# Row maxima taken over every eighth query, with one store in place of a transpose and four, and an earlier load of a key difference

## The reference, cut to what matters

```
scores = einsum('bsdkg,btdk->bkgst', q, k) / sqrt(256)
w      = softmax(scores, axis=-1)
ctx    = einsum('bkgst,btdk->bkgsd', w, v)
```

## Time and profile before

| | us |
|---|---|
| median of 3 runs | 871.83 |
| the profiled execution | 866.55 |
| its span | 864.7 |
| VectorE (DVE) busy | 701.9, 81% of the span |
| TensorE matmul (PE) busy | 776.1, 90% |
| ScalarE (ACT) busy | 537.8, 62% |
| GpSimd (POOL) busy | 330.4, 38% |

### The profile page before, as it was taken

The page is one execution under the profiler, slowest core; times in us unless marked ns, Lnnn a source line. Parts: engine busy times, 40 slices in busy tenths (PEclk is TensorE's granted clock), DMA queues, the critical chain, the costliest instruction groups (busy, mean ns, idle before and its releaser), DMA issues. The chain is left out here.

```text
span 864.7 us, 18013 instructions
## 1 busy us (share of the span) xinstructions
PE 776.1 (90%) x6593; PEld 508.2 (59%) x6593; DVE 701.9 (81%) x1131; ACT 537.8 (62%) x988; POOL 330.4 (38%) x283
## 2 busy tenths in 40 slices
PE   3979999999999999999899998996668899999986
PEld 2865333333333333333388887986657587999875
DVE  4769999999999999999766676668999486666486
ACT  4527788887788888888844335445576353666442
POOL 5440444347544653021010000107787560444340
PEclk9985999999999999999999999998687699999999
DMA  6495532222222222000066000002006113444352
GB/s 240 172 217 165 191 89 52 52 52 53 51 53 52 52 52 52 16 16 17 20 202 127 2 1 13 2 1 70 5 11 270 69 63 60 123 124 134 114 161 74
DMA packets 60183, 71.16 MB, mean 82 GB/s; under 512 B 24864, under 2 KB 46496, under 8 KB 59712
## 3 DMA queue, kind: packets, MB, share of 16 engines
q1 hardware_dynamic: 56016, 59.31, 25.7%
q0 software_dynamic: 3408, 9.38, 3.1%
q10 hardware_dynamic: 672, 1.31, 0.5%
HBM read 40.47 MB, written 27.41 MB: 78 GB/s over the span
## 5 line engine op out<-in xcount | busy, mean ns | idle before, releaser
L767 ACT ACTIVATE probs_t<-psum 128x512 f32<-128x512 f32 x512 | 271.4, 601 | 65.5 <-PE psum L891 63.7
L791 DVE TENSOR_REDUCE row_max<-psum 128x1 f32<-128x1024 f32 x234 | 272.5, 1214 | 10.4 <-PE psum L879 9.9
L891 PE MATMUL psum<-QS,KS 50*128 50x512 f32 x512 | 194.5, 469 | 1.3 <-ACT probs_t L767 1.2
L879 PE MATMUL psum<-KS,QS 48*128 48x512 f32 x490 | 174.2, 457 | 13.6 <-DVE row_max L791 11.3
L701 POOL TENSOR_TENSOR lut_sum<-lut_sum,lut_tmp 128x1080 f32<-128x1080 f32 x45 | 112.3, 2496 | 131.0 <-DVE lut_tmp L822 131.0
L891 PEld LDWEIGHTS psum<-QS,KS 50*128 50x128 f32 x512 | 82.7, 188 | 135.2 <-ACT probs_t L767 127.8
L903 PE MATMUL psum<-probs_t,VS 128*32 128x512 f32 x1024 | 137.9, 611 | 1.1
L879 PEld LDWEIGHTS psum<-KS,QS 48*128 48x128 f32 x490 | 77.3, 195 | 54.0 <-DVE row_max L791 48.3
L2531 POOL DMA_INDIRECT y_rows<-y_slot,ids x39 | 37.5, 962 | 61.4 <-ACT y_slot L2594 61.1
L822 DVE TENSOR_SCALAR lut_tmp<-lut_idx,lut 128x1080 f32<-128x1080 int32 x60 | 47.5, 793 | 0.4
L1289 POOL TENSOR_TENSOR rstd<-var_eps,minus_half 128x4 f32<-128x4 f32 x8 | 8.4, 1045 | 99.9 <-DVE var_eps L1284 99.9
(11 more groups left out here) (333 smaller groups left out, 1902.1 us busy)
## 6 DMA issues: line engine op xcount, KB each, us to landing
KS<-k_rows SPq DMA_DIRECT2D x31, 192.0 KB, 4.5
QS<-q_rows SPq DMA_DIRECT2D x31, 192.0 KB, 5.0
x_rows<-zero_rows SPq DMA_DIRECT2D x1, 4992.0 KB, 17.7
x_slot<-x_rows SPq DMA_DIRECT2D x39, 128.0 KB
m_raw<-experts_w SPq DMA_DIRECT2D x2, 2432.0 KB
q_rows<-part SPq DMA_DIRECT2D x8, 512.0 KB, 5.2
y_token<-y_rows SPq DMA_DIRECT2D x8, 512.0 KB, 7.4
x_tok<-x SPq DMA_DIRECT2D x4, 512.0 KB, 8.8
```

Of the source, the lines that this page charges most:

```text
L767: nc.scalar.activation(pt[:, k % NPT, :], ring(k)[:], ACT.Exp, scale=float(E) ** -0.5).then_inc(p_ready, 1)
L791: nc.vector.tensor_reduce(out, m.psum[:, j:j + 2, :], AX_XY, ALU.max).then_inc(max_done, 1)
L879: mm = nc.tensor.matmul(bank[pair(k) + h], QS[n % NQK][rows(g, NROW), st * P:(st + 1) * P], keys, start=True, stop=True)
L891: nc.tensor.matmul(ring(k)[:], KS[n % NQK][rows(g, NAUG), t * P:(t + 1) * P], QS[n % NQK][rows(g, NAUG), half * BLK:(half + 1) * BLK], sta ...
```

## The change

The maxima of tile st are now those of queries st, st + 8, st + 16 and so on: partition p of column c holds query 8p + c. The stationary operand of a maximum therefore reads QS with a step of eight elements (32 bytes). The maxima of a partition are then 8 neighbouring queries for each head; one DMA stores the parts, and the two loads into QS take 128 pieces of 32 bytes for each row. The transpose and the clearing of `row_max` go; GpSimd works on 16 columns in place of 32. PLAIN goes from 4 to 2. KD[0] of head 0 moves from ScalarE's queue to SyncE's, ahead of `load_qk(1)`, and with it the wait for `kd_out`. `look_up(0)` takes over a wait that `turn_max(0)` had.

```diff
-        m.m_rows = nc.dram_tensor("m_rows", (B * KV, NPART, G * S), ...).ap()
+        m.m_rows = nc.dram_tensor("m_rows", (B * KV, P, NPART, G * S // P), ...).ap()
...
         act.wait_ge(kd_out, 32)
-        m.load_diff(act, 0)
+        m.load_diff(act, 0, (1,))
...
-    FIRST, PLAIN = NST + AHEAD, 4
+    FIRST, PLAIN = NST + AHEAD, 2
...
-    def load_diff(queue, n):
-        for g in range(G):
+    def load_diff(queue, n, heads=range(G)):
+        for g in heads:
...
         queue.wait_ge(mp_done, NPART * (n + 1))
-        for q in range(4):
-            queue.dma_start(m.m_rows[n].rearrange("i (c q s) -> q c i s", q=4, s=32)[q],
-                            mpt[32 * q:32 * q + NST, :, :].bitcast(F32)).then_inc(mp_out, 16)
-        queue.wait_ge(mp_out, 64 * (n + 1))
+        queue.dma_start(m.m_rows[n].rearrange("p i k -> p (i k)"), mpt[:]....bitcast(F32)).then_inc(mp_out, 16)
+        queue.wait_ge(mp_out, 16 * (n + 1))
         for g in range(G):
             queue.dma_start(QS[n % NQK][g * HEAD_ROWS + NROW:g * HEAD_ROWS + NAUG, :].bitcast(F32)
-                            m.m_rows[n, :, g * S:(g + 1) * S]).then_inc(m_in, 16)
+                            .rearrange("i (p c) -> i p c", c=NTT),
+                            m.m_rows[n].rearrange("p i k -> i p k")[:, :, g * NTT:(g + 1) * NTT]).then_inc(m_in, 16)
...
         load_qk(sp, 0, (0,))
+        sp.wait_ge(m.kd_out, 32)
+        load_diff(sp, 0, (0,))
         load_qk(sp, 1)
-        sp.wait_ge(m.kd_out, 32)
         load_diff(sp, 1)
...
-        pool.wait_ge(mt_done, n + 1)
-        nc.gpsimd.tensor_scalar(mres[:, 0, :], mT[:], -1.0, None, ALU.mult).then_inc(mres_done, 1)
+        pool.wait_ge(max_done, NST * (n + 1))
+        nc.gpsimd.tensor_scalar(mres[:], mx[:, n % 2, :], -1.0, None, ALU.mult).then_inc(mres_done, 1)
...
-        def turn_max(n):
-            ...
-            nc.vector.transpose(mT[:], mx[:, n % 2, :]).then_inc(mt_done, 1)
...
-            mm = nc.tensor.matmul(bank[pair(k) + h], QS[n % NQK][rows(g, NROW), st * P:(st + 1) * P], keys,
+            mm = nc.tensor.matmul(bank[pair(k) + h], QS[n % NQK][rows(g, NROW), :]
+                                  .rearrange("r (p c) -> r c p", c=NTT)[:, st], keys,
                                   start=True, stop=True)
```

More of the change, by code:

```diff
@@ L113, in program @@
         m.kd_rows = nc.dram_tensor("kd_rows", (KV * HD, len(K_SLOTS), BLK), F32, kind="Internal").ap()
-        m.m_rows = nc.dram_tensor("m_rows", (B * KV, NPART, G * S), F32, kind="Internal").ap()
+        m.m_rows = nc.dram_tensor("m_rows", (B * KV, P, NPART, G * S // P), F32, kind="Internal").ap()
         m.den_rows = nc.dram_tensor("den_rows", (B * KV, G * S), F32, kind="Internal").ap()
@@ L518, in attention_stage @@
     rec = at("rec_b", [P, 2, S], F32, b); b += 2 * S * 4
[L519 to L522, removed]
+    mx = at("row_max", [P, 2, NST], F32, b); b += 2 * NST * 4
+    mres = at("max_res", [P, NST], F32, b); b += NST * 4
+    mpt = at("max_parts", [P, NPART, NST], F32R, b); b += NPART * NST * 4
     den = at("den", [P, NST], F32, b); b += NST * 4
@@ L543, in attention_stage @@
         sem(n) for n in ("lut_in", "idx_in", "lut_prod", "lut_add", "f_hi", "f_lo"))
-    mx_zero = sem("mx_zero")
-    max_ps, max_done, mt_done, mp_done, mp_out, m_in = (
-        m.front_sem(n) for n in ("max_ps", "max_done", "mt_done", "mp_done", "mp_out", "m_in"))
+    max_ps, max_done, mp_done, mp_out, m_in = (
+        m.front_sem(n) for n in ("max_ps", "max_done", "mp_done", "mp_out", "m_in"))
     m.s_ps = sem("s_ps")
@@ L644, in place_max @@
         queue.wait_ge(mp_done, NPART * (n + 1))
-        for q in range(4):
-            queue.dma_start(m.m_rows[n].rearrange("i (c q s) -> q c i s", q=4, s=32)[q],
-                            mpt[32 * q:32 * q + NST, :, :].bitcast(F32)).then_inc(mp_out, 16)
-        queue.wait_ge(mp_out, 64 * (n + 1))
+        queue.dma_start(m.m_rows[n].rearrange("p i k -> p (i k)"), mpt[:].rearrange("p i k -> p (i k)").bitcast(F32)
+                        ).then_inc(mp_out, 16)
+        queue.wait_ge(mp_out, 16 * (n + 1))
         for g in range(G):
-            queue.dma_start(QS[n % NQK][g * HEAD_ROWS + NROW:g * HEAD_ROWS + NAUG, :].bitcast(F32),
-                            m.m_rows[n, :, g * S:(g + 1) * S]).then_inc(m_in, 16)
+            queue.dma_start(QS[n % NQK][g * HEAD_ROWS + NROW:g * HEAD_ROWS + NAUG, :].bitcast(F32)
+                            .rearrange("i (p c) -> i p c", c=NTT),
+                            m.m_rows[n].rearrange("p i k -> i p k")[:, :, g * NTT:(g + 1) * NTT]).then_inc(m_in, 16)
     def attend_sync(sp):
@@ L711, in max_parts @@
     def max_parts(pool, n):
-        pool.wait_ge(mt_done, n + 1)
-        nc.gpsimd.tensor_scalar(mres[:, 0, :], mT[:], -1.0, None, ALU.mult).then_inc(mres_done, 1)
+        pool.wait_ge(max_done, NST * (n + 1))
+        nc.gpsimd.tensor_scalar(mres[:], mx[:, n % 2, :], -1.0, None, ALU.mult).then_inc(mres_done, 1)
         pool.wait_ge(mres_done, n + 1)
         if n >= 1:
-            pool.wait_ge(mp_out, 64 * n)
-        nc.gpsimd.tensor_copy(mpt[:, 0, :], mres[:, 0, :]).then_inc(mp_done, 1)
+            pool.wait_ge(mp_out, 16 * n)
+        nc.gpsimd.tensor_copy(mpt[:, 0, :], mres[:]).then_inc(mp_done, 1)
         pool.wait_ge(mp_done, NPART * n + 1)
-        nc.gpsimd.tensor_tensor(mpt[:, 1, :], mres[:, 0, :], mpt[:, 0, :], ALU.subtract).then_inc(mp_done, 1)
+        nc.gpsimd.tensor_tensor(mpt[:, 1, :], mres[:], mpt[:, 0, :], ALU.subtract).then_inc(mp_done, 1)
     def attend_gpsimd(pool):
@@ L773, in attend_vector @@
         m.project_vector(dve)
-        nc.vector.memset(mx[:], 0.0).then_inc(mx_zero, 1)
-        dve.wait_ge(mx_zero, 1)
         def row_max(n, i):
@@ L780, in row_max @@
             if i == 0 and n >= 2:
-                dve.wait_ge(mt_done, n - 1)
+                dve.wait_ge(mres_done, n - 1)
             col = i % G * NTT + i // G
@@ L816, in look_up @@
                 dve.wait_ge(max_done, FIRST)
+                dve.wait_ge(m.part_lo, 3 * NB)
             if (c + 1) * PIECE > KC * GUW and v == 0:
@@ L826, in attend_vector @@
             row_max(i // NST, i % NST)
-            if i == NST - 1:
-                turn_max(0)
         for n in range(NG):
@@ L833, in attend_vector @@
                     row_max(k // NST, k % NST)
-                    if k % NST == NST - 1:
-                        turn_max(k // NST)
                 if i == 12 and n >= 1:
```

## The result

The changed kernel took 863.54 us (median of 6, 861.63 to 866.89) against 870.80 for the kernel before (median of 6): the means of the same runs have the ratio 0.993, interval 0.9906 to 0.9955. (All ratios in this document are ratios of means, so they differ a little from what the medians give.) In two later comparisons, on two chips, the same two kernels stood at 865.80 against 871.01 us (0.9950, interval 0.9927 to 0.9973) and 853.24 against 856.36 (0.9961, interval 0.9936 to 0.9985). So the change is faster by 0.4 to 0.7%, 3 to 7 us. The predicted 864.8 us is 1.3 off. The way there was right in front and wrong in the steady part.

What follows compares the result with a forecast made beforehand. VectorE was taken to bound steady attention, with a front hole waiting for KD[0]. Gains 4.4 + 2.9 - 0.3 = 7.0 us took the 871.83 us median to 864.8, range 858 to 871.5 (8 in 10).

Steps and rivals of the forecast that it cites:

- KD[0] earlier: Front of attention: KD[0] lands at 56 us, so maxima alone would let scores begin 4.9 us earlier, at 74.5.
- The way into QS: Group 0 maxima, store and loads: load takes 4.0 us over two engines, scores begin at 75.0, gain 4.4 us; later groups hidden.
- (c): Loads into QS: all pieces on one engine, total 867.5 us; chance 0.06.
- (d): Loads into QS: from 25 ns a piece every group's scores wait; near 900 us at 35 ns; chance 0.06.
- The transpose: VectorE, steady attention: removing 15 transposes of 0.212 us gains 2.9 us, ends 1.5 and 3.5.
- The strided load: Maximum matmuls on TensorE: weight loads with a 32-byte step mostly hide behind the matmul before, costing 0.3 us.
- Rival (e): Maximum weight loads: from 0.32 us a load they decide; steps grow 0.5 us, total near 920; chance 0.06.
- The clock: TensorE's clock in the front: expected still at 0.50 from 60 to about 84 us.
- Rival (a): Relu stretch: without the hole TensorE's clock holds 2.4 GHz, about 3.8 us more gained, 861.0 us; chance 0.14.
- the sum's 7.0 us: Whole kernel: total gain forecast, 4.4 + 2.9 - 0.3 us; chance of the forecast 0.58.

Runs made afterwards that it cites:

- e8: Kernel before with only the early KD[0] and PLAIN = 2, plus both matmuls of each relu maximum issued twice: 855.15 us, ratio 0.9966.
- e10: Changed kernel with no step in the weight load, ordering done in the store (4096 pieces of 4 bytes), 4 KB rows loaded: 1055.16 us, ratio 1.2313.
- e3: Changed kernel with no step in the maxima's weight load, so maxima reaching QS belong to other queries: 862.95 us, ratio 0.9928.
- e4: Changed kernel unaltered, run again for a same-chip comparison and second trace: 865.80 us, ratio 0.9950 against the kernel before.
- e12: Changed kernel unaltered, run again on another chip as yardstick, third trace: 853.24 us, ratio 0.9961 against the kernel before.
- e2: Changed kernel with KD[0] loaded as before and PLAIN = 4, leaving only the new layout of the maxima: 869.35 us, ratio 0.9989.
- e9: Changed kernel with a step of two in the weight load, ordering done in the store (2048 pieces of 8 bytes), 4 KB rows loaded: 854.54 us, ratio 0.9972.
- e7: Changed kernel with SyncE waiting for group 0's two loads into QS before its next DMA: 854.82 us, executed once.
- e5: Changed kernel with a weight-load step of two elements (8 bytes), maxima reaching QS belonging to other queries: 847.93 us, one execution.
- e6: Changed kernel with a weight-load step of four elements (16 bytes), maxima reaching QS belonging to other queries: 855.70 us, one execution.

## Why the prediction was right or wrong

1. **KD[0] earlier.** Right. Landed at 57.0 where 56 was taken; the relu form started at 58.76 (58.6), 23 maxima at 0.69 us put the scores at 74.62 (75.0), the gain there was 4.8 us (4.4), with 73.1 to 74.9 in the other traces of this front (without e8 to e10, which delay the scores in other ways).
2. **The way into QS.** The mechanism was right, two engines for the loads, and the size was off: 3.15 us or less in place of 4.0, at 6 ns a piece and not 10. It never decided. Rivals (c) and (d) are out for the load; scores that wait for the maxima in every group, as in (d), came with the small pieces of the store (e10).
3. **The transpose, 2.9 us.** This step failed. It took VectorE's busy share as proof that VectorE alone set the pace. e3 took the transpose away with contiguous loads and won 0.05 to 0.08 us a group, about 1 us in all: TensorE is so close behind that the maxima start late, by 0.15 us a group more than before. So an instruction taken off VectorE was not "time saved".
4. **The strided load, 0.3 us.** This term was mis-sized. It costs 0.23 us a group, 15 groups: 3.5 us. The doubled load was reckoned hidden, since a load waited 45.7 us for VectorE in sum; in the timeline the second matmul of a pair follows the first after 0.47 us (177.53, 178.00) in place of 0.34:

```profile
177.53 0.63 PE L864 MATMUL psum<-KS,QS 48*128 48x512 f32 x1
...
178.00 0.78 PE L864 MATMUL psum<-KS,QS 48*128 48x512 f32 x2
```

   Rival (e) named the right place with far too high a price. Its sum with the measured load, (4 x (0.324 - 0.213) - 0.41) x 112, gives 3.8 us, near the 3.5; but 20.1 us of the loads' waiting were left, so it was the tightest places that decided and not the mean room.
5. **The clock.** The forecast had it rise some ten us after the first scores, as before. It rose 11 to 19 us after them, since the end of the slow stretch did not move with the scores (it came at 85 to 94 us, before at 90), and group 0 grew from 22.9 us to between 23.4 and 26.0. This is 0.5 to 3.1 us of the front's gain given back, a term that the sum lacked. Rival (a) fell: the hole was closed, and the clock fell nevertheless.

So the sum's 7.0 us came near the first measurement (7.3 us by the medians) by luck: the two later comparisons gave 5.2 and 3.1 us. The traces give less. The front wins 4.8 to 5.9 us, the clock in group 0 takes back 0.5 to 3.1, and the longer groups take 15 x 0.17 = 2.6; the second drop of the clock, in some executions only, moves the end by another 1 to 3. Attention ended at 426.1 us in the trace of before, and at 427.4, 422.3 (e4) and 421.5 (e12) in three of the changed kernel: 1.2 us later, 3.8 and 4.6 sooner.

The medians say 3 to 7. Part of the difference is that the one trace of before is of a quick execution. Another part goes with the clock. On the chip of e4, 31 executions of before have a mean granted clock of 0.943 and the twelve of the changed kernel 0.947, and in both sets the time falls by about 5 us for each 0.01 of clock (correlation -0.76 and -0.80). By this estimate some 2 of the 5 us there go with a higher clock. Whether the change brings that or chance does, and where in the program, is not shown: e2, which has the late front, also stands at 0.947.

## What to carry to other kernels

A busy share of 99% names the engine that is late, not the one that is next: before an instruction is taken off it, look in the timeline how far the feeding engine is ahead at the tightest place. When a layout change makes a weight load strided, price the load; here a step of two fp32 elements was nearly free and one of four was not. When a transfer must reorder small pieces, look at what its store and its load each cost until they are complete, not only at how long the engines move bytes. Undo each half of a change by itself: here one half carried the gain, and the other cost 1.6 to 1.9 us by the medians.

## What the runs showed of the hardware

A store of small pieces into DRAM completes long after its pieces are recorded. With 2048 pieces of 8 bytes the DMA engines are busy for 1.3 us and at rest for 5.1 more before the store counts as complete; with 4096 pieces of 4 bytes it is 8.0 and 7.8 us (e9, e10). From issue to landing that is 7.4 and 17.2 us, where 512 pieces of 32 bytes out of DRAM landed within 3.15 us (e7). The weight load of 128 fp32 columns has a knee between steps of 8 and 16 bytes: 193 and 317 ns (e5, e6). TensorE's clock stayed at 1.2 GHz through 12 us in which TensorE was busy all the time by its rows (80 to 92 us of the changed kernel), rose at different times in traces of the same kernel (93, 88 and 85 us), and was not held by more matmuls (e8, 21 in place of 13 in 4 us). And chips differ outside of the change: the changed kernel's attention ends at 422.3 us in e4 and 421.5 in e12, and the rest takes 438.5 us on the one chip and 426.7 on the other.
